# A gated delta rule between two recurrent layers on one core: eight sets of small products per block, issued as four pairs

## The chip, the cores and the metric

The kernel runs on one NeuronCore of a Trainium2 chip, in FP32. The metric is the device time of one execution in microseconds. Engines: PE is TensorE (its weight loads are shown apart, as PEld), ACT is ScalarE, DVE is VectorE, POOL is GpSimd, SP is SyncE, which issues the transfers.

## The reference

The input x is 8 x 1024 x 256 (B sequences, L places, D features). It goes through three residual steps: x + 0.5 ffn(ln(x)), then x + attn(ln(x)), then x + 0.5 ffn(ln(x)) with the same weights.

- `ffn` is a gated recurrence along the first axis, the 8 sequences: f = sigmoid(x wf' + c uf' + bf), i = sigmoid(x wi' + c ui' + bi), g = tanh(x wc' + c uc' + bc), c = f c + i g, and at the end tanh(x wo' + c_final uo' + bo). Each of the 1024 places is a lane of its own, so 8 steps in order are all that is sequential.
- `attn` is a gated delta rule along the 1024 places, for 8 x 16 heads of width 16: with k the RMS-normed input per head and v the negative of x W', per place S = lam S; S += beta k (v - k'S); o = k'S. Then a layer norm with weights over the sum of x W' and o.

## The kernel before, in words

**Blocks.** The 1024 places are cut into 8 blocks of 128 (NB). Block b holds 128 places on the partitions and 8 sequences, so one pass of the ffn recurrence over a block takes 8 steps (TILE, t = 0 to 7). A step of the ffn is 24 matrix products of 128x128 by 128x128 on PE (L445): 12 of the input (XMM), and 12 of the state (CMM), of which the last 12 wait for the state of the step before (`c_done`, L443). ScalarE makes the gates from PSUM (L462, L469), VectorE the new state (L484, L488, L490). An FP32 product shows in the trace as two PE records, so these 12 products are x24, a half of them x12.

**The chunked delta rule.** The recurrence of `attn` is made chunk by chunk, 16 places each. For a block, spread over the steps of the blocks behind it: transposes (lt, L665), the value products (v, L675), key rows and their transposes (kt, L684), gram products (g0 to g3, L704, 64 records each half), their transposes (gt, L839), a triangular solve on VectorE (inv1 to inv3, L790 and L793), transposes of the inverse (tt, L851), evicted by L822 on ScalarE and L801 on VectorE, and then the applied inverse: eight sets, ta0 to ta7 (L868). A set is 64 products of 32x32 by 32x32, 128 records, into one PSUM bank: sets with an even number go to bank 6 and are evicted by ScalarE (L829), those with an odd number to bank 7 and by VectorE (L808), both into `xs_out`, which SP stores at steps 0 (sets 0 to 3) and 4 (sets 4 to 7) (L914). The operands of a set stand on 32 partitions (`tok`); an even set and the odd one behind it use neighbouring strips of 32 partitions. The four products of an inner loop go to the four column strips:

```
for k in [4 * "abcd".index(part) + r for part in parts for r in range(4)]:
    for c in range(SETS):
        lane = SETS * (16 * kh + k) + c
        mm = pe.matmul(dst.ps[32 * c:32 * c + 32, 32 * k:32 * k + 32],
                       kv_of(n)[tok, lane, :], invT[tok, lane, :], ...)
```

**Two stages.** The first stage (`first_*`) runs blocks 0 to 5 of the first ffn (SOLO = 6), steps 0 to 47, up to about 474 us. The second (`second_*`) runs everything else, steps 48 to 130: the last two blocks of the first ffn, the 8 blocks of the second, and beside them the 64 hops of the delta rule's state, one per step from step 49 on. A hop is 32 products with the state (L1058), a copy by ScalarE (L1084), 32 products that make the new state (L1075), and five evictions into `zbd` (L1092 on ScalarE, L1099 on VectorE).

**The order around the change is a table written by hand.** `PERIOD` lists for each step t four parts, and for each part the items that go there, each with the number of blocks it lies behind the current one; `CLOSE` lists those behind step 7. All engines walk the same table, each doing its own share of an item, in the table's order. Where a part lies on PE differs by stage. In the first, part 0 lies between the two halves of XMM, part 1 behind XMM and ahead of CMM, part 2 between the halves of CMM, part 3 behind CMM; ScalarE and VectorE do the items of parts 0 to 2 ahead of their share of the step and those of part 3 behind it. In the second stage CMM is issued first, around the hop, and the four parts each stand behind 3 products of XMM of the next step; ScalarE and VectorE do all four parts behind their share of the step. At the block's end (`CLOSE`, the first stage) PE issues the output products h0 to h3 (L512), the term of the final state (L497) and the transposes of the next block (L405), and VectorE evicts them (L520, L526, L537), takes the statistics of the next layer norm (L83) and evicts the last gram sets (L630).

Sets 0 to 3 of a block come two blocks behind (steps 5, 5, 6 and the close), sets 4 to 7 three blocks behind (steps 1, 2, 2, 3). `fill_table` walks the same table and gives each PSUM bank the order in which it is filled; PE waits with `refill` for the bank's last eviction. A set waits for its bank, the first one also for `inv_cols`, the keys and the values (L856 to L861).

Of the kernel before, what the change touches and what calls it, by code (L numbers as in the profile page):

```python
# [130 lines left out]
class Bank:  # L131


    def __init__(self, k, ps, sem):
# [1 line left out]


PERIOD = {0: ([], [(2, "g3abcd")], [], [(1, "ln2_late")]),
# [7 lines left out]
CLOSE = ([], [(2, "ta3abcd")], [], [(1, "g2abcd")])  # L146
S_PIECES = (4, 5)
GRAMS = ("g0", "g1", "g2", "g3")
UNITS = tuple(f"ta{m}" for m in range(8))
# [26 lines left out]
def fill_table():  # L176
# [11 lines left out]
    def singles(banks, *keys):  # L188
        for key in keys:
            k = turn.get(banks, 0)  # L190
            put(banks[k % len(banks)], *key)
            turn[banks] = k + 1
# [6 lines left out]
    def four(name, n, js=range(4)):  # L199
        return [(name, n, j) for j in js]  # L200

    def piece(name, n):
        name, parts = unit_of(name)
        if not 0 <= n < NB or (parts and "a" not in parts):
            return
        if name[:2] in ("gt", "tt", "lt", "kt"):
            singles((4, 5), *four(name[:2], n, pair_of(name)))
        elif name == "al":
            singles((4, 5), ("al", n))
        elif name in ("v01", "v23"):  # L210
            singles((4, 5), *four("v", n, (0, 1) if name == "v01" else (2, 3)))
        elif name in GRAMS:
            pairs((6, 7), ("g", n, int(name[1])))
        elif name in UNITS:
            m = int(name[2])
            put(6 + m % 2, "ta", n, m)

    singles((4, 5), *four("fr1", 0))
    for b in range(SOLO):
# [8 lines left out]
        for part in range(4):  # L228
            if part == 2:
                singles((4, 5), *four("fr1", b + 1, (0, 1)))  # L230
            for behind, name in CLOSE[part]:
                piece(name, b - behind)
        singles((4, 5), ("ct1", b))
    for i in range(JOIN, END):
# [10 lines left out]
        if t == TILE - 1:  # L245
            for part in range(4):
                if part == 2 and n + 1 < NB:
                    singles((4, 5), *four(*(("fr1", b + 1) if n + 1 < 0 else ("fr2", n + 1)), (0, 1)))
                for behind, name in CLOSE[part]:
                    piece(name, b - behind)  # L250
# [5 lines left out]
def build(nc, x, weights, cols, rows, lanes, out):  # L256
    ctx = ExitStack()
    with ctx:
# [619 lines left out]
        def pieces(eng, b, names, prep, solve):  # L878

            for behind, name in names:  # L880
                if 0 <= b.n - behind < NB:
                    prep(eng, b.n - behind, name)
                    solve(eng, b.n - behind, name)
# [52 lines left out]
        def first_dve(dve):  # L936
            for b in blocks(SOLO):
                for t in range(8):
# [5 lines left out]
                    pieces(dve, b, PERIOD[t][3], prep_dve, solve_dve)  # L944
                pieces(dve, b, CLOSE[1], prep_dve, solve_dve)
                ff.dve_cterm(dve, b)
# [5 lines left out]
                ff.dve_h(dve, b, 3)  # L952
                pieces(dve, b, CLOSE[3], prep_dve, solve_dve)
                ff.dve_x(dve, b, 2)
# [9 lines left out]
        def first_pe(pe):  # L964
            for b in blocks(SOLO):
# [13 lines left out]
                ff.pe_h(pe, b, 0)  # L979
                pieces(pe, b, CLOSE[0], prep_pe, solve_pe)  # L980
                ff.pe_h(pe, b, 1)
                pieces(pe, b, CLOSE[1], prep_pe, solve_pe)
                ff.pe_front(pe, b.ahead(1), (0, 1))
# [571 lines left out]
```

## Time and profile before

| | us |
|---|---|
| Median of 3 runs | 1371.61 |
| Runs | 1363.80 to 1374.17 |
| The profiled execution, its own time | 1371.25 |
| Its span, first to last instruction | 1369.5 |
| PE busy / PEld busy | 1263.5 / 1167.3 |
| DVE busy / ACT busy / POOL busy | 878.1 / 666.4 / 269.5 |

The durations come from the one profiled execution, taken by the hardware profiler. Busy time is the union of an engine's instructions; matmuls are pipelined and their ends modelled, so the distance from one start to the next says more than a duration. In brackets behind a row of the timeline stands how long the engine was idle before it and who released it; "issue" means that nothing in the profile ended the wait. The granted clock (PEclk) is TensorE's, as a share of full speed. A row of the windows gives the stretch, its length, then busy time and number of instructions for PE, PEld, DVE, ACT and POOL, the granted clock, the mean busy share of the DMA engines and GB/s. A row of a queue gives packets, MB and the share of time of the 16 DMA engines.

### The profile page before, as it was taken

How to read it: one execution, taken by the hardware profiler on the slowest of the kernel's cores; microseconds unless marked ns; L12 is line 12 of the kernel's file. 1: busy time of each engine (PE TensorE's matmuls, PEld its weight loads, DVE VectorE, ACT ScalarE, POOL GpSimd, SP SyncE). 2: the span in 40 equal slices, each digit the busy share in tenths (PEclk: the TensorE clock that was granted, in tenths of full speed). 3: DMA queues.
4: the chain of work that ended last, by engine and by line, in shares of the span. 5: the costliest groups of instructions: out<-in, count | busy, mean ns of one | idle time of the engine just before them, and what ended most of it. 6: DMA issues, size and time to landing. Idle time of an engine off the chain costs nothing.

```text
span 1369.5 us, 58093 instructions
## 1 busy us (share of the span) xinstructions
PE 1263.5 (92%) x25763; PEld 1167.3 (85%) x25763; DVE 878.1 (64%) x2147; ACT 666.4 (49%) x1623; POOL 269.5 (20%) x350
## 2 busy tenths in 40 slices
PE   6999999999999999998898899899899999999896
PEld 5989998989989888787777788888789989898886
DVE  3656886868879676577658764953445546464632
ACT  3244444454434535544463555355365756655432
POOL 0113112021311111112503230230130405050500
PEclk9999999999999999999998999999999999999999
DMA  4010201122121223242214223324234233333000
GB/s 146 1 62 32 65 33 66 64 80 73 42 80 50 102 68 92 67 140 66 83 47 162 65 74 117 92 77 138 73 95 150 65 112 102 109 102 108 1 32 31
DMA packets 72378, 108.36 MB, mean 79 GB/s; under 512 B 12352, under 2 KB 49472, under 8 KB 70080
## 3 DMA queue, kind: packets, MB, share of 16 engines
q1 hardware_dynamic: 72128, 104.65, 23.9%
q8 instruction: 203, 3.33, 1.0%
q14 instruction: 47, 0.39, 0.1%
HBM read 53.74 MB, written 50.86 MB: 76 GB/s over the span
## 4 chain that ended last, share of the span: by engine, by line
PE 67%; DVE 18%; ACT 8%; issue 5%; DVEq 0%; ACTq 0%
PE ps L445 37%; PE ps L512 7%; PE ps L868 5%; PE ps L1058 4%; PE ps L1075 3%; ACT gates L462 3%; PE ps L675 3%; ACT zbd L1092 2%; DVE prod L790 2%; DVE inv L793 2%; DVE ln_bn L83 2%; PE ps L405 2%; PE ps L704 1%; DVE hs L526 1%; DVE ffn_rows L537 1%
## 5 line engine op out<-in xcount | busy, mean ns | idle before, releaser
L445 PE MATMUL ps<-cst,wt 128*128 128x128 f32 x2688 | 348.7, 282 | 3.5 <-DVE cst L490 3.4
L445 PEld LDWEIGHTS ps<-cst,wt 128*128 128x128 f32 x2688 | 318.7, 194 | 14.6 <-DVE cst L490 4.1
L445 PE MATMUL ps<-ffn_rows,wt 128*128 128x128 f32 x2304 | 295.7, 281 | 10.8 <-DVE hs L526 4.1
L445 PEld LDWEIGHTS ps<-ffn_rows,wt 128*128 128x128 f32 x2304 | 275.9, 194 | 20.8 <-issue 13.2
L462 ACT ACTIVATE gates<-ps,colv 128x128 f32<-128x128 f32 x448 | 128.0, 369 | 188.7 <-PE ps L445 188.5
L484 DVE TENSOR_TENSOR fc<-gates,cst 128x256 f32<-128x256 f32 x112 | 56.1, 501 | 223.5 <-ACT gates L462 223.5
L1161 POOL TENSOR_TENSOR ffn_rows<-ffn_rows,rowv 128x256 f32<-128x256 f32 x64 | 52.0, 851 | 351.3 <-DMA ffn_rows<-x_scratch 351.3
L1092 ACT ACTIVATE zbd<-ps,mask 32x256 f32<-32x256 f32 x252 | 104.0, 458 | 10.7 <-PE ps L1075 7.6
L868 PE MATMUL ps<-inv_cols,kv 32*32 32x32 f32 x8192 | 88.7, 194 | 18.5 <-issue 16.9
L868 PEld LDWEIGHTS ps<-inv_cols,kv 32*32 32x32 f32 x8192 | 79.2, 104 | 30.5 <-issue 20.9
L445 PE MATMUL ps<-kg_rows,wt 128*128 128x128 f32 x768 | 95.1, 278 | 6.6 <-DVE hs_more L526 3.5
L445 PEld LDWEIGHTS ps<-kg_rows,wt 128*128 128x128 f32 x768 | 89.2, 192 | 10.3 <-issue 5.8
L512 PE MATMUL ps<-wt,ffn_rows 128*128 128x256 f32 x384 | 91.8, 384 | 5.8 <-DVE hs L526 3.0
L1084 ACT COPY e<-ps 128x512 f32<-128x512 f32 x64 | 37.5, 585 | 118.9 <-PE ps L1058 118.9
L1058 PE MATMUL ps<-zbd,xsb 128*32 128x64 f32 x4096 | 86.3, 239 | 7.4 <-issue 7.3
L83 DVE BATCH_NORM_STATS2 ln_bn<-ffn_rows 128x6 f32<-128x256 f32 x256 | 86.6, 411 | 9.2 <-DMA ffn_rows<-x 8.7
L1058 PEld LDWEIGHTS ps<-zbd,xsb 128*32 128x32 f32 x4096 | 75.9, 149 | 19.3 <-issue 14.2
L488 DVE TENSOR_TENSOR ig<-gates 128x256 f32<-128x256 f32 x128 | 61.3, 479 | 44.7 <-ACT gates L469 41.7
L101 POOL TENSOR_SCALAR key_rows<-ffn_rows,ln_stats 128x256 f32<-128x256 f32 x64 | 39.2, 628 | 256.5 <-PE ps L839 207.1
L512 PEld LDWEIGHTS ps<-wt,ffn_rows 128*128 128x128 f32 x384 | 70.0, 190 | 17.5 <-ACT gates L462 4.2
L650 POOL TENSOR_TENSOR kg_rows<-key_rows,g_tok 128x512 f32<-128x512 f32 x32 | 47.2, 1501 | 188.1 <-DVE key_rows L604 188.1
L1099 DVE TENSOR_TENSOR zbd<-ps,mask 64x1024 f32<-64x1024 f32 x63 | 76.2, 1210 | 7.6 <-PE ps L1075 7.6
(123 smaller groups left out, 1793.7 us busy)
## 6 DMA issues: line engine op xcount, KB each, us to landing
xs_scratch<-xs_out SPq DMA_DIRECT2D x32, 512.0 KB, 3.5
xsb<-xs_scratch SPq DMA_DIRECT2D x256, 64.0 KB
ffn_rows<-x SPq DMA_DIRECT2D x32, 256.0 KB, 3.6
x_scratch<-ffn_rows SPq DMA_DIRECT2D x32, 256.0 KB, 2.8
kg_scratch<-kg_rows SPq DMA_DIRECT2D x32, 256.0 KB, 2.8
kgb<-kg_scratch SPq DMA_DIRECT2D x256, 32.0 KB, 2.3
e_scratch<-e SPq DMA_DIRECT2D x256, 32.0 KB
ffn_rows<-e_scratch SPq DMA_DIRECT2D x8, 1024.0 KB
```

The source lines that it names most:

```text
L83: link(dve.bn_stats(stats[:, b, 0:6], src[:, b, :]))
L445: mm = pe.matmul(banks[g][:, col:col + P], wt[:, w, k, m * P:(m + 1) * P], rhs, start=(x in (0, FI)), stop=(k == KT - 1 and (t == 0 or x > ...
L462: a = act.activation(gates[q][:, g, m * P:(m + 1) * P], fi[:, g * D + m * P:g * D + (m + 1) * P], ACT.Sigmoid, bias=bias[:, g, m:m + 1])
L484: a = dve.tensor_tensor(fc, gates[q][:, 0, :], cst, ALU.mult)
L488: dve.tensor_tensor(ig, gates[q][:, 1, :], gates[q][:, 2, :], ALU.mult).then_inc(self.products, 1)
L512: mm = pe.matmul(h_b[j][:, e * D:(e + 1) * D], self.xnT[b.n % len(self.xnT)][:, k, 2 * j + e, :], wt[:, WO, k, :], start=(e == 0 and k == ...
L650: pool.tensor_tensor(kg_rows.rearrange("p (b h d) -> p b h d", h=H, d=HD)[:, 2 * r:2 * r + 2, :, :], key_rows.rearrange("p (b h d) -> p b ...
L868: mm = pe.matmul(dst.ps[32 * c:32 * c + 32, 32 * k:32 * k + 32], kv_of(n)[tok, lane, :], invT[tok, lane, :], start=True, stop=True, skip_g ...
L1058: mm = pe.matmul(E_BANK[32 * g:32 * g + 32, 64 * kk:64 * kk + 64], xs_cols[:, k // C, k % C, C * a:C * a + 2 * C], zbd[:, k, :], start=Tru ...
L1092: act.activation(zbd[rows, C:2 * C, cols], S_BANKS[rows, :, cols], ACT.Copy, scale=mask4[rows, c:c + 1]).then_inc(z_done, 1)
L1099: dve.tensor_tensor(zbd[0:64, 0:C, :].rearrange("p k (c d) -> p k c d", c=SETS), S_BANKS[0:64, :, :].rearrange("p k (c d) -> p k c d", c=S ...
L1161: pool.tensor_tensor(xt[p][:, r, :], xt[p][:, r, :], rowv[:, 2, :], ALU.add).then_inc(post_done, 1)
```

## The change

The sets are issued two at a time, at one place of a step. Sets 4 and 5 come in part 1 of step 1, sets 6 and 7 in part 2 of step 2, sets 0 and 1 in part 2 of step 5, sets 2 and 3 in part 1 of step 6. The block's close and step 3 have none left. Nothing else of the table is changed; the products, the banks, the evictions and the transfers are the same ones, and each engine's share of an item moves with it.

```
 PERIOD = {0: ([], [(2, "g3abcd")], [], [(1, "ln2_late")]),
-          1: ([(2, "gt0")], [(3, "ta4abcd"), (1, "lc2")], [], [(2, "gt1"), (2, "inv1"), (1, "apply")]),
-          2: ([(3, "ta5abcd")], [], [(3, "ta6abcd")], [(1, "lt0"), (2, "inv2")]),
-          3: ([(1, "lt1"), (1, "square")], [(3, "ta7abcd")], [(2, "al")], [(1, "v01"), (2, "inv3")]),
+          1: ([(2, "gt0")], [(3, "ta4abcd"), (3, "ta5abcd"), (1, "lc2")], [], [(2, "gt1"), (2, "inv1"), (1, "apply")]),
+          2: ([], [], [(3, "ta6abcd"), (3, "ta7abcd")], [(1, "lt0"), (2, "inv2")]),
+          3: ([(1, "lt1"), (1, "square")], [], [(2, "al")], [(1, "v01"), (2, "inv3")]),
           4: ([(1, "v23"), (1, "sums")], [(1, "rms")], [(2, "tt0")], [(2, "tt1"), (1, "key")]),
-          5: ([(1, "keys")], [(2, "ta0abcd")], [], [(2, "ta1abcd"), (-1, "ln1")]),
-          6: ([(1, "kt0")], [(2, "ta2abcd"), (1, "km0")], [], [(1, "kt1"), (-1, "lc1")]),
+          5: ([(1, "keys")], [], [(2, "ta0abcd"), (2, "ta1abcd")], [(-1, "ln1")]),
+          6: ([(1, "kt0")], [(2, "ta2abcd"), (2, "ta3abcd"), (1, "km0")], [], [(1, "kt1"), (-1, "lc1")]),
           7: ([(1, "g0abcd"), (-1, "ap0")], [], [(1, "g1abcd"), (-1, "ap1")], [(1, "km1")])}
-CLOSE = ([], [(2, "ta3abcd")], [], [(1, "g2abcd")])
+CLOSE = ([], [], [], [(1, "g2abcd")])
```

## Rows read from the trace of the kernel before

**Rows 1.** The page: busy time by engine, and the instruction queue.

```profile
PE 1263.5 (92%) x25763; PEld 1167.3 (85%) x25763; DVE 878.1 (64%) x2147; ACT 666.4 (49%) x1623; POOL 269.5 (20%) x350
...
q8 instruction: 203, 3.33, 1.0%
```

**Rows 2.** Windows: first stage from 226 us, then the stretch with sets and hops.

```profile
226.00:474.00 248.00, 239.22 (x5275) 223.71 (x5274) 197.72 (x468) 113.73 (x267) 47.80 (x60) 1.00 0.20 69
474.00:985.00 511.00, 459.72 (x12092) 415.70 (x12096) 334.03 (x749) 255.49 (x589) 100.06 (x124) 0.95 0.29 91
```

**Rows 3.** Waits of PE: total us, times, longest.

```profile
PE ps L868 <- issue: 16.9, 14, 3.4
...
PE ps L851 <- DVE inv_cols L801: 8.7, 4, 3.2
PE ps L1058 <- issue: 7.3, 6, 2.6
```

**Rows 4.** Timeline of PE, second stage, sets 5 and 6: start, us, instruction.

```profile
501.36 0.27 PE L868 MATMUL ps<-inv_cols,kv 32*32 32x32 f32 x9 [0.27 <-issue]
501.56 1.60 PE L445 MATMUL ps<-ffn_rows,wt 128*128 128x128 f32 x12
503.09 1.10 PE L868 MATMUL ps<-inv_cols,kv 32*32 32x32 f32 x107
505.38 0.38 PE L868 MATMUL ps<-inv_cols,kv 32*32 32x32 f32 x21 [1.19 <-issue]
```

**Rows 5.** The same for the last block's sets 5 and 6.

```profile
965.35 0.45 PE L868 MATMUL ps<-inv_cols,kv 32*32 32x32 f32 x31 [0.85 <-issue]
965.73 1.60 PE L445 MATMUL ps<-ffn_rows,wt 128*128 128x128 f32 x12
967.27 0.92 PE L868 MATMUL ps<-inv_cols,kv 32*32 32x32 f32 x85
971.56 0.85 PE L868 MATMUL ps<-inv_cols,kv 32*32 32x32 f32 x43 [3.38 <-issue]
```

**Rows 6.** Timeline of PE, first stage, sets 5 and 6.

```profile
237.64 1.29 PE L868 MATMUL ps<-inv_cols,kv 32*32 32x32 f32 x128
238.85 1.60 PE L445 MATMUL ps<-ffn_rows,wt 128*128 128x128 f32 x12
240.30 1.50 PE L445 MATMUL ps<-cst,wt 128*128 128x128 f32 x12
241.73 0.55 PE L868 MATMUL ps<-inv_cols,kv 32*32 32x32 f32 x40
242.59 0.95 PE L868 MATMUL ps<-inv_cols,kv 32*32 32x32 f32 x88 [0.31 <-issue]
```

**Rows 7.** Timeline of PE, first stage, step 4, away from the sets.

```profile
346.64 1.50 PE L445 MATMUL ps<-cst,wt 128*128 128x128 f32 x12
347.98 1.06 PE L851 MATMUL ps<-ident,inv 128*128 128x128 f32 x8
```

**Rows 8.** Window at half clock, columns as in rows 2, to 755.73 us.

```profile
748.91:755.73 6.82, 6.82 (x155) 6.25 (x142) 6.62 (x11) 2.45 (x4) 4.36 (x6) 0.50 0.06 13
```

**Rows 9.** Timeline of PE, second stage, behind two other sets.

```profile
732.43 2.93 PE L445 MATMUL ps<-ffn_rows,wt 128*128 128x128 f32 x12
735.15 1.10 PE L839 MATMUL ps<-ident,key_rows 128*128 128x128 f32 x8
...
748.68 1.15 PE L868 MATMUL ps<-inv_cols,kv 32*32 32x32 f32 x77 [3.13 <-issue]
```

**Rows 10.** Timeline, first stage: the new state of step 1, its products in step 2.

```profile
320.81 0.67 DVE L490 TENSOR_TENSOR cst<-fc,ig 128x256 f32<-128x256 f32 x1
...
324.34 1.50 PE L445 MATMUL ps<-cst,wt 128*128 128x128 f32 x12
```

**Rows 11.** Timeline, first stage, block's end: VectorE's first item, and PE behind its last.

```profile
385.45 0.42 DVE L520 TENSOR_TENSOR cterm<-ps,rowv 128x256 f32<-128x256 f32 x1 [2.85 <-PE ps L497]
...
396.02 1.14 PE L839 MATMUL ps<-ident,key_rows 128*128 128x128 f32 x8 [1.43 <-DVE key_rows L630]
```

## The prediction

> **What bounds the kernel now.** I read the page's busy rows first, then the windows by stage, then TensorE's timeline, and last the chain of waits for the two kinds of idle time that it has.
>
> TensorE (PE) is busy 1263.5 us of a span of 1369.5 us; the next engine, VectorE, 878.1 us [rows 1]. The share is high in both stages: 239.2 of 248 us (96%) in the first stage from 226 us on, where the sets run without hops, and 459.7 of 511 us (90%) in the stretch where sets and hops run together [rows 2]. So PE's own order sets the time, and a moved item on PE costs or gives what it adds to or takes from PE's queue. What fills PE's idle time differs: in the first stage it is a few waits for VectorE and ScalarE at a block's seam, in the second it is first of all "issue" before the lines of the change (L868, 16.9 us in 14 waits) and of the hop (L1058, 7.3 us in 6) [rows 3]. "Issue" means that the engine had no semaphore to wait for. The change lies on that line, so this is what I look at closest.
>
> What stands behind it: the instruction queue brought 203 packets and 3.33 MB [rows 1], 16.4 KB a packet. PE ran 25763 matmuls and 25763 weight loads, 51526 instructions; 3.33 MB over these is 64.6 bytes each, and 51526 / 203 is 254. So I read that queue as PE's own code, and a packet as a page of about 256 instructions, 128 matmul records with their loads. One set is 128 records, so a set is one page of code.
>
> The idle times have exactly that spacing. PE idles for issue inside a set at 501.36, then runs 9 + 12 + 107 = 128 records, and idles for issue again until 505.38 [rows 4]. It resumes at 965.35, runs 31 + 12 + 85 = 128, and idles until 971.56 [rows 5]. In both a set is followed by only 12 ordinary records and then the next set. A page was entered at 501.36 and the next one only at 505.38: 4.0 us; the other took 6.2 us (965.35 to 971.56). In the first stage the wait at 242.59 lies 40 + 12 + 12 + 64 records behind a point halfway through the set at 237.64, about 238.2: 4.4 us a page, and there only 0.31 us of it shows, because 24 ordinary records lie between the two sets [rows 6]. I take from this: the next page is asked for when the present one is entered, and is there about 4 us later (6 where transfers are dense); a page that is run faster than that ends in a wait.
>
> **The change part by part.** Per block eight sets become four pairs, 32 merges in all.
>
> *Merged switches (gain).* A group of 12 ordinary records takes 1.34 us between its own kind (346.64 to 347.98) [rows 7]; 1.43 us when a set follows (240.30 to 241.73) and 1.45 after a set (238.85 to 240.30), and the set itself 1.21 us (237.64 to 238.85) [rows 6]. A lone set so costs 1.21 + 0.09 + 0.11 = 1.41 us. The second set of a pair has ordinary records on neither side: between 1.0 us (it also loses the hand-over at its end) and 1.21. A merge saves 0.2 to 0.4, I take 0.3: 32 x 0.3 = 10 us. The step from one set to the next in another row strip and PSUM bank is not in this trace; if it cost as much as a switch the gain is 0, so this term is 0 to -13 us.
>
> *A whole page inside a pair (loss).* A pair is 256 records, 512 instructions, so wherever the pages fall at least one lies wholly in the pair. It is run in 1.2 us and the next page comes 4.0 us after its entry: 2.8 us of wait. PE's queue takes code a little ahead of the array, so I use 2.5 in the first stage, where also fewer transfers run (69 GB/s against 91 [rows 2]). Its bounds are 0.3 us (the wait at 242.59, were the queue to cover the rest) and 5.0 (6.2 - 1.2). First stage: sets 0 to 3 of four blocks and sets 4 to 7 of three, 8 + 6 = 14 pairs: +35 us. The waits that it has now there (0.3 us seen at L868) are worth 1 us.
>
> Second stage: 18 pairs. There the page price is 4.0 to 6.2, and the pair stands among two hop groups of 64 records each; I take 3.1 us a pair, 56 us. Against that stands what is there now: L868 16.9 less the 0.3 of the first stage and L1058 7.3 make 24 us [rows 3], since sets 5 and 6 and sets 0 and 1 are already 12 records apart in this stage, near to a pair. Net +32. PE now waits 8.7 us in all for VectorE's eviction at L801 [rows 3], at the end of its solve of the block; a PE that is late finds part of this gone: -4. Bounds of this term: +5 (the near pairs are as bad as pairs, only steps 1 and 6 get worse, by 1 us each) to +60 (5.0 a pair).
>
> *The clock (loss).* Over 474 to 985 the granted clock is 0.95 [rows 2], and it falls to 0.50 for some 3.4 us at a time after waits of this kind: the stretch from 748.91 on is at 0.50 [rows 8], right after the wait of 3.13 us that ended at 748.68, and the group of 12 that starts at 732.43 behind another set needs 2.72 us, to 735.15 [rows 9], where 1.45 is usual [rows 6]. The first stage has 1.00 [rows 2]. Half speed costs 1.3 us for one such group, and 1.7 for a whole stretch of 3.4 us. With a pair and its wait of 2.5 us in one piece I expect most pairs to end so. New are 14 in the first stage and 9 in the second (steps 1 and 6; the other 9 pairs stand where near pairs stand now and have such stretches already). Not each will fall on ordinary records: 23 x 0.9 = 21 us. Bounds 0 and 23 x 1.7 = 39.
>
> *Covers that get shorter (nothing).* Set 5 leaves step 2 ahead of the recurrent products. Now the state is written at 321.48 (320.81 + 0.67) and those products start at 324.34 [rows 10]; without the set's 1.41 us some 1.4 us of that remains, and the eviction of set 5, which now comes ahead of VectorE's coefficients in step 1, must fit in there. Set 3 leaves the block's end; VectorE starts there with the term at 385.45, which waits 2.85 us for PE, and works from there up to the gram eviction that PE awaits at 396.02 [rows 11], so PE and VectorE move ahead together and that wait stays at 1.43 us. Sets 1 and 7 are evicted a half step earlier, between waits for the gates. Were one of these covers gone, I put it at 1 us a block, 8 us. No DMA moves: the stores of the sets stay at steps 0 and 4.
>
> *Sum against the profiled run:* 1371.25 us (span 1369.5 and 1.75 around it), which is the median of the runs, 1371.61, to 0.03%. 1371.25 - 10 + 35 - 1 + 32 - 4 + 21 = 1444 us.
>
> **A rule that speaks against this.** The Trainium skill, "Runtime: NRT & Kernel Launch", section on instruction fetch mechanics, has the same page, 16 KiB or 256 instructions, fetched while the present one runs, but says that crossing a page is mostly hidden, and gives PE room for 2048 instructions. By it the pair's 512 instructions would be there ahead and only the merges would count. The waits of rows 4 and 5, one page apart, say otherwise.
>
> **The rivals.**
> 1. *Merges alone: faster.* PE's code is ahead by more than a pair, and the waits at L868 have another cause that goes with the hop. For it: the first stage runs its lone sets with almost no issue wait. Against it: 128 records between two waits, twice, and a wait at 242.59 without a hop near. It decides from the point where two pages are ready at a pair's start. Time: 1371.25 - 10 = 1361. The page of the skill named above is the rule for this one.
> 2. *Waits, but short and without the clock.* PE takes code far enough ahead that a pair waits 1.0 to 1.5 us, and such waits leave the clock at 1.00. For it: near pairs 12 records apart wait as little as 1.19 us (at 505.38). Against it: those 12 records gave PE 1.5 us of other work, and others wait 3.38 us all the same [rows 4, 5]. Time, with 5 us for a clock that falls here and there: 1371.25 - 10 + 32 x 1.2 - 4 + 5 = 1401.
> 3. *Pages at 6 us everywhere.* The fetch is as slow in steps 1, 2 and 6 of each stage, where the block's loads and stores are issued, as at 971.56. Time: 1371.25 - 10 + 14 x 3.8 + 18 x 4.5 - 24 - 4 + 30 = 1497.
> 4. *A tie.* Waits of some 0.3 us a pair eat the merges' gain: 1371.25 - 10 + 10 = 1371.
>
> **How the numbers follow.** The forecast has 0.74 (own range 1410 to 1475), rival 1 0.03, rival 2 0.12, rival 3 0.08, rival 4 0.03. About 1% is what a measurement can tell here, so faster is below 1357.9 and slower above 1385.3: 0.03 faster, 0.03 the same, 0.94 slower. The range leaves out most of rivals 1, 3 and 4 and the low end of rival 2: 1396 to 1484 us.
>
> **What would show it right or wrong.** In the changed profile: issue waits before L868 in nearly all 32 pairs, 2 to 3 us each, 70 to 100 us together, also before 474 us, where there is 0.3 now; successive waits 128 records apart; the first stage's granted clock below 1.00; a block of the first stage with four pairs some 10 us longer. Of the merge: 12-record groups between the old places of the sets back at 1.34 us. It is wrong if the pairs run through in 2.3 us without a break, or if the added time stands before L445 with VectorE as the releaser (a cover gone), or if the waits come but are under 1.5 us.

## The result and the profile after

The changed kernel takes 1464.9 us (median of 4 runs, 1461.8 to 1470.5) against 1370.3 us: a ratio of 1.0725, 95% interval 1.0683 to 1.0767. It is slower, as forecast, and by more: 95 us where 73 were forecast, inside the range of 1396 to 1484 us.

The page of the changed kernel answers to [rows 1]: the same numbers of instructions, the same 203 packets of code, PE busy for 1307.4 us instead of 1263.5, in a span that is 99.2 us longer.

```profile
span 1468.7 us, 58093 instructions
...
PE 1307.4 (89%) x25763; PEld 1214.5 (83%) x25763; DVE 864.8 (59%) x2147; ACT 668.7 (46%) x1623; POOL 267.8 (18%) x350
...
q8 instruction: 203, 3.33, 0.9%
```

The waits of PE (total us, times, longest), to set beside [rows 3]:

```profile
PE ps L868 <- issue: 75.7, 34, 4.4
...
PE ps L851 <- DVE inv_cols L801: 8.7, 4, 3.2
...
PE ps L665 <- DVE zbd L1099: 5.0, 3, 2.2
...
PE ps L1058 <- issue: 2.7, 2, 1.7
```

Issue waits inside the sets went from 16.9 us in 14 to 75.7 us in 34. The first stage alone (25 us to the first hop at 536.7) shows it without anything beside it, since it had one wait of 0.3 us there:

```profile
PE ps L868 <- issue: 30.6, 15, 2.6
```

Two of its pairs in PE's timeline: first set 5 beside set 4, with the ordinary records behind it, then sets 6 and 7.

```profile
337.85 2.42 PE L868 MATMUL ps<-inv_cols,kv 32*32 32x32 f32 x228
342.62 0.64 PE L868 MATMUL ps<-inv_cols,kv 32*32 32x32 f32 x28 [2.35 <-issue]
343.19 3.14 PE L445 MATMUL ps<-cst,wt 128*128 128x128 f32 x13
...
353.20 1.54 PE L868 MATMUL ps<-inv_cols,kv 32*32 32x32 f32 x159
357.17 1.02 PE L868 MATMUL ps<-inv_cols,kv 32*32 32x32 f32 x97 [2.43 <-issue]
358.12 2.93 PE L445 MATMUL ps<-cst,wt 128*128 128x128 f32 x12
360.84 1.38 PE L665 MATMUL ps<-ident,key_rows 128*128 128x128 f32 x8
```

The 256 records of a pair come as 228 + 28 or 159 + 97: no break where the second set begins, at 128, but one at another place each time. From one of the 14 long waits of this stage to the next PE runs 256, 762, 256, 507, 255, 763, ... records, close to a multiple of 127 or 128 each time (51526 instructions in 203 packets are 254 each, 127 records with their loads).

The trace also keeps the packets of the instruction queue one by one, 16384 bytes each. In this stage such a packet ends inside each of the 14 long waits, and PE resumes 1.2 to 1.6 us behind its end. The wait that ends at 342.62 has a packet from 340.39 to 341.31, the wait that ends at 357.17 one from 354.77 to 355.86. So the spacing is not the only sign that these waits are for code.

The group of 12 behind the second pair takes 2.72 us (358.12 to 360.84), where a group behind a set takes 1.45 in [rows 6]. The windows say why: at both pairs a stretch at half clock follows, which in the first of them begins inside the wait. The last two rows are the block of the first stage around them, 98.8 us, and the same block before, 83.4 us: 15.4 us more for four pairs.

```profile
341.00:347.80 6.80, 5.17 (x49) 5.11 (x50) 3.31 (x21) 0.79 (x4) 0.00 (x0) 0.50 0.01 2
358.10:361.50 3.40, 3.40 (x26) 3.38 (x17) 1.18 (x2) 1.55 (x6) 0.00 (x0) 0.50 0.02 5
324.90:423.70 98.80, 87.83 (x1791) 83.08 (x1790) 65.04 (x159) 39.13 (x90) 15.21 (x20) 0.91 0.16 56
...
302.00:385.40 83.40, 81.18 (x1790) 75.98 (x1790) 66.88 (x158) 38.52 (x90) 15.94 (x20) 1.00 0.19 67
```

**Where the 99 us are.** The windows split the two traces, the kernel before first, at the first hop. In the first stage (25 us to the first hop):

```profile
25.00:481.70 456.70, 440.14 (x7828) 414.10 (x7827) 344.59 (x865) 205.66 (x501) 84.51 (x108) 1.00 0.16 56
```

```profile
25.00:536.70 511.70, 466.31 (x7811) 441.84 (x7809) 335.80 (x865) 206.64 (x497) 82.25 (x108) 0.93 0.14 50
```

It is 55.0 us longer, 28.8 us of it PE idle (511.7 - 466.3 against 456.7 - 440.1) and 26.2 us PE busy with the same work. From the first hop to the last set, again before and after:

```profile
481.70:982.20 500.50, 449.51 (x11839) 406.20 (x11841) 324.70 (x713) 251.26 (x578) 100.06 (x124) 0.95 0.30 92
```

```profile
536.70:1074.00 537.30, 459.05 (x11792) 417.87 (x11791) 320.86 (x711) 247.16 (x567) 96.93 (x119) 0.90 0.27 85
```

Idle time rose from 51.0 to 78.3 us, by 27.3. (The last set now stands a step earlier than before, so the lengths of these windows aren't compared; from the first hop to the end the span is 44.2 us longer: 1468.7 - 536.7 against 1369.5 - 481.7.) Together: 56 us of idle time and 43 us of slower work.

### The profile page after: what moved, and what is told of

It reads as the page before. It is cut to its first block, busy times and chain, and to the rows that moved or that the text cites. A ratio compares the mean times of both kernels' runs of the same rounds, so it can differ in the third digit from the quotient of the medians.

```text
span 1468.7 us, 58093 instructions
## 1 busy us (share of the span) xinstructions
PE 1307.4 (89%) x25763; PEld 1214.5 (83%) x25763; DVE 864.8 (59%) x2147; ACT 668.7 (46%) x1623; POOL 267.8 (18%) x350
## 4 chain that ended last, share of the span: by engine, by line
PE 68%; DVE 16%; issue 8%; ACT 7%; DVEq 0%; ACTq 0%
PE ps L445 39%; PE ps L512 6%; PE ps L868 5%; PE ps L1058 4%; PE ps L1075 3%; PE ps L675 3%; ACT gates L462 2%; DVE prod L790 2%; DVE inv L793 2%; ACT zbd L1092 2%; DVE ln_bn L83 2%; PE ps L704 1%; PE ps L405 1%; DVE hs L526 1%; PE ps L684 1%
## 5 line engine op out<-in xcount | busy, mean ns | idle before, releaser
L445 PE MATMUL ps<-cst,wt 128*128 128x128 f32 x2688 | 372.1, 294 | 3.4 <-DVE cst L490 3.4
L445 PEld LDWEIGHTS ps<-cst,wt 128*128 128x128 f32 x2688 | 341.3, 205 | 14.5 <-DVE cst L490 4.1
L445 PE MATMUL ps<-ffn_rows,wt 128*128 128x128 f32 x2304 | 304.7, 287 | 10.9 <-DVE hs L526 4.1
L445 PEld LDWEIGHTS ps<-ffn_rows,wt 128*128 128x128 f32 x2304 | 286.9, 201 | 20.1 <-issue 13.0
L484 DVE TENSOR_TENSOR fc<-gates,cst 128x256 f32<-128x256 f32 x112 | 52.3, 467 | 250.1 <-ACT gates L462 250.1
L868 PE MATMUL ps<-inv_cols,kv 32*32 32x32 f32 x8192 | 91.4, 199 | 75.7 <-issue 75.7
L868 PEld LDWEIGHTS ps<-inv_cols,kv 32*32 32x32 f32 x8192 | 83.4, 109 | 83.6 <-issue 79.5
L445 PE MATMUL ps<-kg_rows,wt 128*128 128x128 f32 x768 | 97.9, 284 | 6.6 <-DVE hs_more L526 3.5
L445 PEld LDWEIGHTS ps<-kg_rows,wt 128*128 128x128 f32 x768 | 91.9, 197 | 10.3 <-issue 5.8
L1058 PEld LDWEIGHTS ps<-zbd,xsb 128*32 128x32 f32 x4096 | 77.5, 151 | 16.0 <-issue 11.6
L1058 PE MATMUL ps<-zbd,xsb 128*32 128x64 f32 x4096 | 87.7, 244 | 2.9 <-issue 2.7
L1099 DVE TENSOR_TENSOR zbd<-ps,mask 64x1024 f32<-64x1024 f32 x63 | 76.2, 1209 | 6.2 <-PE ps L1075 6.2
```

Of the source, the lines that this page charges most:

```text
L445: mm = pe.matmul(banks[g][:, col:col + P], wt[:, w, k, m * P:(m + 1) * P], rhs, start=(x in (0, FI)), stop=(k == KT - 1 and (t == 0 or x > ...
L484: a = dve.tensor_tensor(fc, gates[q][:, 0, :], cst, ALU.mult)
L1058: mm = pe.matmul(E_BANK[32 * g:32 * g + 32, 64 * kk:64 * kk + 64], xs_cols[:, k // C, k % C, C * a:C * a + 2 * C], zbd[:, k, :], start=Tru ...
L1099: dve.tensor_tensor(zbd[0:64, 0:C, :].rearrange("p k (c d) -> p k c d", c=SETS), S_BANKS[0:64, :, :].rearrange("p k (c d) -> p k c d", c=S ...
```

## The experiments

Kernels in which a table differs by stage have a second copy of `PERIOD` and `CLOSE`, and so 9 is added to the line numbers: L877 is L868, L1067 is L1058, L454 is L445, L674 is L665, L1108 is L1099. "First stage" below is 25 us to the first hop.

**The pairs of one stage alone.** Do the two stages add up? First with the changed table for blocks 0 to 5 only (the code in outline):

```
 for b in range(SOLO): ... PERIOD[t][part], CLOSE[part]      # changed table
 for i in range(JOIN, END): ... PERIOD2[t][part], CLOSE2[part]   # old table
```

Expected: 

> The changed table for blocks 0 to 5 (first stage), the old one behind them: 14 of the 32 pairs. Code pages and clock: each of the 14 pairs waits 2.1 to 2.6 us for code and is followed by a half-clock stretch, as in the changed kernel's first stage, where the first hop came 55 us later; 1370 + 55 = 1425 us, and the second stage as before, with its 24 us of issue waits. If the pairs of the first stage shift what the second stage waits for, it is off this by more than 8 us.

Measured: 1425.9 us (ratio 1.041, 1.037 to 1.046), the first hop at 535.5 us against 481.7. In its first stage:

```profile
PE ps L877 <- issue: 30.4, 15, 2.5
```

The other way round, `PERIOD` old and `PERIOD2` changed:

Expected: 

> The old table for blocks 0 to 5, the changed one behind them: 18 of the 32 pairs. If the two stages add up, this has what the first stage's pairs do not explain: 1370 + 97 - 55 = 1412 us, first stage at clock 1.00 without an issue wait, waits at L868 some 45 us.

Measured: 1413.7 us (1.030, 1.024 to 1.036). The two extras, 56 and 44 us, make 100 where the whole change has 95. So the stages add up within the intervals, which are 7 to 8 us wide on either side: 14 pairs cost 4.0 us each and 18 pairs 2.4 us each, and no effect of one stage on the other is seen. In the second kernel the waits inside the sets behind the first hop are close to the changed kernel's: 44 us against 45.

**Half the code in each set.** In `solve_pe`, with the old table and then with the changed one:

```
-for k in [4 * "abcd".index(part) + r for part in parts for r in range(4)]:
+for k in [4 * "abcd".index(part) + r for part in parts if part in "ab" for r in range(4)]:
```

A set is then 64 records, and a pair of them 128; these kernels leave out the other half of the applied inverse. Expected of the sets one by one: 

> The old table, and every set computes only its first half (32 products, 64 records, half a page of code); the other half of the applied inverse is left out. Code pages: 64 sets are 0.55 us shorter (-35), and since two sets 12 records apart are now less than a page together, nearly all issue waits of the second stage go (-20) and with them most half-clock stretches (-15): 1300 us. Rival (two sets close to each other disturb the array or PSUM itself, whatever their code): only the 35 us go, 1335 us, and the waits at L868 stay near 17 us.

Expected of the pairs: 

> The changed table with the same half sets: a pair is one page of code instead of two; the other half of the applied inverse is left out. Code pages: hardly any page lies wholly in a pair, so the waits at L868 fall from 76 us to under 15, and the merges show alone: 10 us less than the half sets one by one, about 1290 us. Rival (the step from one set to the next in another row strip and bank is what waits): 32 waits of 2.3 us and their clock stay, some 90 us above the half sets one by one, about 1390 us.

Measured: 1323.2 us one by one, 1323.7 us as pairs (ratios to before 0.966, 0.961 to 0.971, and 0.968, 0.962 to 0.973). The rival's 1390 us for the pairs is excluded: with the same places, the same 32 steps to another row strip and bank and half the code, the 95 us are gone. This alone does not say whether the code or the halved work took them away; the four sets in a row below do. PE's timeline of the half-size pairs, two of them with the records around them:

```profile
302.66 1.50 PE L445 MATMUL ps<-ffn_rows,wt 128*128 128x128 f32 x12
304.10 1.31 PE L868 MATMUL ps<-inv_cols,kv 32*32 32x32 f32 x128
305.34 2.94 PE L445 MATMUL ps<-cst,wt 128*128 128x128 f32 x24
...
311.70 1.50 PE L445 MATMUL ps<-cst,wt 128*128 128x128 f32 x12
313.13 1.31 PE L868 MATMUL ps<-inv_cols,kv 32*32 32x32 f32 x128
314.37 1.60 PE L445 MATMUL ps<-cst,wt 128*128 128x128 f32 x12
```

A pair of half sets runs in 1.24 us without a break, 0.03 us more than one whole set of 128 records in [rows 6]: the change of strip and bank costs nothing to speak of. For the worth of a merge I compare the first stages, one by one and then as pairs:

```profile
25.00:465.90 440.90, 425.23 (x6031) 399.17 (x6030) 343.50 (x865) 205.16 (x501) 84.42 (x108) 1.00 0.17 58
```

```profile
25.00:462.20 437.20, 419.38 (x6019) 395.97 (x6017) 341.12 (x863) 204.19 (x495) 84.31 (x108) 1.00 0.17 58
```

PE is busy 5.85 us less over 14 merges, 0.42 us each, and 2.1 us of that is waited again. But my expectation of both kernels missed by 23 and 34 us, and the two were to differ by 10: in the second stage the gain does not reach the end. From the first hop on the pairs even take 7.2 us more than the sets one by one (859.6 against 852.4). These waits of PE for VectorE in the kernel one by one have grown most:

```profile
PE ps L665 <- DVE zbd L1099: 19.4, 3, 9.1
...
PE ps L844 <- DVE zbd L1099: 5.8, 1, 5.8
```

Before, L665 waited 3.7 us for that and L844 1.0, so 20.5 us are new. In the second stage a PE that comes early to step 3 waits for VectorE's share of the hop, which stands behind the solve in VectorE's queue (L790 and L793 from 716.2 to 725.2 ahead of L1099 at 725.47, where the wait of 9.1 us ends). In three of the four blocks in which the half sets wait there the old kernel does too, for 0.9 to 2.7 us. My reading is that its issue waits ahead of that place (2.78 us in step 2 of one block, 3.13 in that of the next) only shortened this wait and cost nearly nothing; no run takes them away by themselves.

**A near pair: 12 ordinary records between the two sets.** First stage only.

```
-          1: ([(2, "gt0")], [(3, "ta4abcd"), (3, "ta5abcd"), (1, "lc2")], [], ...
+          1: ([(2, "gt0")], [(3, "ta4abcd"), (1, "lc2")], [(3, "ta5abcd")], ...
...
+          2: ([], [(3, "ta6abcd")], [(3, "ta7abcd")], ...
+          5: ([(1, "keys")], [(2, "ta0abcd")], [(2, "ta1abcd")], ...
+          6: ([(1, "kt0")], [(2, "ta2abcd"), (1, "km0")], [(2, "ta3abcd")], ...
```

(The line with a minus is the changed kernel's.)

Expected: 

> First stage only: the same four places, but 12 ordinary records between the two sets of a pair (sets 4 and 5 in parts 1 and 2 of step 1, and so on); the second stage as before. Code pages: the page now holds 12 ordinary records and takes 2.4 us instead of 1.1, so the wait is 3.6 - 2.4 = 1.2 us instead of 2.4: 14 x 1.2 = +17, and a clock that falls in half of the cases +9: 1396 us. Rival (sets in a row wait for the array): no wait and no fall of the clock in the first stage, 1370 us.

Measured: 1386.3 us (1.012, 1.008 to 1.017), the first hop 19.0 us later than before. The rival's 1370 lies outside the interval. The waits of the first stage, and one of its near pairs:

```profile
PE ps L877 <- issue: 12.3, 15, 1.7
```

```profile
333.81 1.29 PE L877 MATMUL ps<-inv_cols,kv 32*32 32x32 f32 x128
335.03 1.60 PE L454 MATMUL ps<-cst,wt 128*128 128x128 f32 x12
336.56 0.45 PE L877 MATMUL ps<-inv_cols,kv 32*32 32x32 f32 x31
338.06 1.02 PE L877 MATMUL ps<-inv_cols,kv 32*32 32x32 f32 x97 [1.05 <-issue]
```

The wait stands at 128 + 31 records, as in the pair at 353.20, and has 1.05 us instead of 2.43: the 12 records took 1.4 us of it. So the wait is about what is missing to a fixed time per page, as expected (0.9 us a pair against 1.2). The clock did less than expected: the first stage has 0.99, with three stretches of 3.4 us at half clock at 14 pairs.

```profile
25.00:500.70 475.70, 447.00 (x7821) 419.57 (x7819) 338.85 (x865) 206.68 (x501) 82.85 (x108) 0.99 0.16 54
```

**Four sets in a row.** First stage only, sets 4 to 7 in part 2 of step 2 and sets 0 to 3 in part 1 of step 6:

```
+          2: ([], [], [(3, "ta4abcd"), (3, "ta5abcd"), (3, "ta6abcd"), (3, "ta7abcd")], ...
+          6: ([(1, "kt0")], [(2, "ta0abcd"), (2, "ta1abcd"), (2, "ta2abcd"), (2, "ta3abcd"), (1, "km0")], ...
```

Expected: 

> First stage only, four sets in a row at two places of a block (sets 4 to 7 in part 2 of step 2, sets 0 to 3 in part 1 of step 6), 7 places in all; the second stage as before. Code pages: 512 records are four pages, so three pages are run in 1.1 us each and each is followed by a wait of 2.4 us: 21 waits, 50 us of idle time before the first hop against 29 with the 14 pairs; with some 18 us of half clock and 6 us for the merges the time is 1370 + 62 = 1432 us. Rival (one wait for each place where sets stand in a row, however many): 7 waits, 16 us, with 12 us of half clock 1370 + 22 = 1392 us.

Measured: 1428.1 us (1.045, 1.042 to 1.048). The rival's 1392 is excluded. The waits of its first stage, and one of the seven places:

```profile
PE ps L877 <- issue: 41.8, 21, 2.7
```

```profile
346.77 1.54 PE L877 MATMUL ps<-inv_cols,kv 32*32 32x32 f32 x159
350.51 1.85 PE L877 MATMUL ps<-inv_cols,kv 32*32 32x32 f32 x128 [2.21 <-issue]
354.24 1.85 PE L877 MATMUL ps<-inv_cols,kv 32*32 32x32 f32 x128 [1.88 <-issue]
357.69 1.51 PE L877 MATMUL ps<-inv_cols,kv 32*32 32x32 f32 x97 [1.60 <-issue]
```

This is the clearest picture of the mechanism. There are 21 waits at 7 places, as the pages have it, and exactly 128 records, 256 instructions, between two of them. In each of the 21 a packet of the instruction queue ends 1.3 to 1.5 us before PE resumes. From one wait's end to the next 3.73 us pass (350.51 to 354.24) and 3.45 us (354.24 to 357.69). The waits were smaller than my 2.4 us, since the later ones find the sets themselves slower (1.85 us for 128 records, not 1.31): that fills part of the same time. That the total came within 4 us of the expectation is luck in part: in the first stage idle time rose by 40 us instead of 50, and PE's busy time by 20.5 instead of 12.

```profile
25.00:542.20 517.20, 460.67 (x7825) 436.31 (x7824) 344.81 (x865) 207.14 (x501) 84.44 (x108) 0.91 0.14 50
```

**Four half sets in a row.** The same places with the half sets.

Expected: 

> The same places with half sets (32 products each; the other half of the applied inverse is left out): four half sets in a row are 256 records, as much code as one pair of whole sets. Code pages: one wait of 2.4 us at each of the 7 places, 17 us of idle time in the first stage, each with a half-clock stretch (some 10 us together), less the merges: 1323 + 22 = 1345 us. If the number of sets in a row counted and not their code, it would be three waits at each place, as with the whole quads: 50 us, 1385 us; with none at all 1318 us.

Measured: 1355.6 us (0.991, 0.988 to 0.994), against 1323.2 for the half sets one by one. The waits of its first stage and one of its places:

```profile
PE ps L877 <- issue: 11.4, 7, 2.0
```

```profile
328.67 1.31 PE L877 MATMUL ps<-inv_cols,kv 32*32 32x32 f32 x128
330.22 0.45 PE L877 MATMUL ps<-inv_cols,kv 32*32 32x32 f32 x31 [0.23 <-ACT xs_out L838]
332.50 1.37 PE L877 MATMUL ps<-inv_cols,kv 32*32 32x32 f32 x97 [1.83 <-issue]
333.79 2.93 PE L454 MATMUL ps<-cst,wt 128*128 128x128 f32 x12
```

Seven issue waits, one per place, with four sets in each: the code counts, not the sets. A pair of whole sets, which is as much code, has one wait as well. As two sets use each bank here, the third and fourth sets also wait for an eviction: the third 0.2 us each time (1.6 in all, L838), the fourth at three places (3.2 us in all, L817). The time is 10 us above the expectation. This stage is 29.4 us longer than with half sets one by one (first hop 495.3 against 465.9); 15.3 us of that is idle time (31.0 against 15.7, with the 4.8 us for the banks in it) and 14.1 us PE busy for longer, with a half-clock stretch at all seven places.

**Sets spread wider than before.** The opposite of the change, second stage only:

```
+          0: ([], [(2, "g3abcd")], [], [(1, "ln2_late"), (3, "ta4abcd")]),
+          1: ([(2, "gt0")], [(1, "lc2")], [(3, "ta5abcd")], ...
+          2: ([], [(3, "ta6abcd")], [], ...
+          3: ([(1, "lt1"), (1, "square")], [(3, "ta7abcd")], ...
+          5: ([(1, "keys")], [(2, "ta0abcd")], [], [(-1, "ln1")]),
+          6: ([(1, "kt0"), (2, "ta1abcd")], [(1, "km0")], [], [(2, "ta2abcd"), (1, "kt1"), ...
```

Expected: 

> The opposite of the change, in the second stage only: no two sets close to each other (set 4 in part 3 of step 0, 5 in part 2 of step 1, 6 in part 1 of step 2, 7 in part 1 of step 3, 0 in part 1 of step 5, 1 in part 0 and 2 in part 3 of step 6, 3 at the close). Code pages: the issue waits of the second stage fall from 26 to about 10 us and the half-clock stretches from 49 us to about 20: 1370 - 16 - 12 = 1342 us. If code is not the cause: 1370 us, within 1%.

Measured: 1390.9 us (1.015, 1.010 to 1.019): a miss by 49 us, and slower. Its waits from the first hop to the last set:

```profile
PE ps L1067 <- issue: 18.9, 10, 4.1
PE ps L674 <- DVE zbd L1108: 18.1, 3, 8.7
...
PE ps L853 <- DVE zbd L1108: 5.6, 1, 5.6
...
PE ps L877 <- issue: 2.4, 5, 0.7
```

The waits left the sets (2.4 us, from 16.6) and went to the hop (18.9, from 6.9): I had moved sets to the end of steps, next to the hop's own dense code, and a page doesn't ask whose code it is. PE also waits 23.7 us for VectorE's `zbd` here, 19 us more than before and most of the added time: the same wait that the half sets showed.

**A smaller attempt.** Second stage only, sets 0 and 1 one part earlier in step 5:

```
-          5: ([(1, "keys")], [(2, "ta0abcd")], [], [(2, "ta1abcd"), (-1, "ln1")]),
+          5: ([(1, "keys"), (2, "ta0abcd")], [], [(2, "ta1abcd")], [(-1, "ln1")]),
```

Expected: 

> An attempt to beat the old order, second stage only: sets 0 and 1 of step 5 stand one part earlier (parts 0 and 2 instead of 1 and 3), so that 6 more ordinary records lie between set 1 and the next hop's code. Code pages: of the 5 us of waits at or behind set 1 in this stage 2 to 3 go, and a half-clock stretch or two: 1370 - 5 = 1365 us, hardly to be told from no change.

Measured: 1369.5 us, ratio 1.001 (0.999 to 1.004): no difference. No order that was tried beats the old one.

## Why the prediction was right, and where it was off

**The merges** gain what was said, somewhat more: 0.42 us each against 0.3, 13 us in all if the second stage's are worth the same. That the step between the two sets might cost a switch was a bound; the half-size pairs show 0.03 us for it. The sign that the forecast named has come too. At the old place of set 5, between the halves of XMM, the 24 records now take 2.68 us, 1.34 for 12:

```profile
349.09 2.84 PE L445 MATMUL ps<-ffn_rows,wt 128*128 128x128 f32 x24
351.77 1.50 PE L445 MATMUL ps<-cst,wt 128*128 128x128 f32 x12
```

**The whole page inside the pair** is shown. All 14 pairs of the first stage wait, the break stands on the page's spacing and not where the sets meet, a packet of code ends shortly before each wait does, half the code takes the waits away, 12 ordinary records between the sets shorten them by the time of these records, four sets in a row have three waits and four half sets have one. The size was near: the changed kernel's idle time is 28.8 us longer in the first stage (forecast 35 less 1) and 27.3 in the second (forecast 32 less 4), 56 against 62. A pair of the first stage waits 2.2 us where I took 2.5. In the second stage the waits at L868 and L1058 went from 24 to 48 us, 2.7 a pair against 3.1, so 24 us net against 32; the price is lower net because the old kernel pays there already. The 4 us that PE's lateness was to take from its wait for VectorE's eviction (L801) did not come: 8.7 us in 4 waits, before and after.

**The clock** is the term that was mis-sized: 21 us forecast. In the first stage PE's busy time rose by 26.2 us although the merges took 5.85 away, so 32 us go to slower work; in the second stage 44.2 us less 27.3 of idle time and plus 7.5 for its 18 merges leave 24. That makes 56 us, 2.7 times the forecast and above its upper bound of 39. The clock's part is what is left when the rest is taken away, not measured by itself; the rows agree with it. The granted clock of 0.93 over 511.7 us means 0.07 x 511.7 / 0.5 = 72 us at half speed, 5.1 us a pair, where I had counted at most one stretch of 3.4 a pair and 0.9 us for it. All 14 pairs have such a stretch, and at six of them it is 6.8 us long, as at 341.00. By the same reckoning the second stage went from 50 to 107 us at half speed, more than nine new pairs at 5.1 us would add, so the pairs that I took as paid for already fell deeper as well. 56 - 21 is 35 us too little, of which the waits (6 too much) and the merges (3 too little) take back 9: 26, the distance from the forecast 73 to the profile's 99. So the total is inside the range although this term is not inside its own, because the terms for the waits came out lower and the merges gained more.

**The covers** held: PE's waits for the new state (L445 for `cst`, 2.8 us in the first stage in both traces) and for the gram eviction (L839, 5.7 us in both, 1.4 at the longest) didn't move. "Time before L445 with VectorE as the releaser" did not come.

**The rivals.** Merges alone and a tie were wrong: their only support, that lone sets in the first stage run without waits, is what the page time makes of 24 ordinary records between two sets. The short waits without the clock had the wrong size in both parts. Pages at 6 us everywhere came at a few places only (the last pair waited 4.42 us). There the packet itself is as short as elsewhere but starts late: 0.94 us long and 3.5 us behind the entry of the page before (counted back 128 records), where the median of the first stage's 14 is 0.9 us. In the old kernel's wait of 3.38 us it is 0.94 us long and 3.8 us late. What held it up is not shown.

**The rule of the Trainium skill** ("Runtime: NRT & Kernel Launch", instruction fetch mechanics) is borne out in the page of 16 KiB or 256 instructions (packets of 16384 bytes, 128 records apart) and in fetching the next page while one runs. Its remarks that the crossing is mostly hidden, and that PE's store has room for 2048 instructions, don't fit a wait at each page of the four sets in a row: here a page that runs in 1.3 to 1.9 us is followed by 1.4 to 2.7 us of wait.

**What stays open:** whether the clock falls for the wait, for the small products around it, or only for both together. The old kernel has a wait of 2.10 us between ordinary products before 474.29 with a granted clock of 1.00 on both sides; half-size pairs, with one issue wait of 0.2 us in all, don't lower it in the first stage (1.00); the pairs of the changed kernel, with waits of 1.5 to 2.6 us, do at all 14. The length of the wait alone does not decide it: of two near pairs with waits of 1.69 and 1.70 us only the first is followed by half clock, while the four half sets in a row, with issue waits of 1.1 to 2.0 us, have it at all seven places. But those also wait for their banks, and no run sets a wait among small products against one among ordinary ones at the same length.

## What to carry to other kernels

Count the instructions on PE, not only its time: each record of a small product is two instructions with its weight load, and where 256 instructions in a row ran faster than that, the next 256 came mostly 3.2 to 4 us after them here, and up to 6.2 us in the stage with more transfers. So dense small products want ordinary, long ones between them, about 24 records of 128x128x128 per 128 small ones (with 24 the first stage had one wait of 0.3 us, with 12 it had 0.9 us a pair). Saving 0.4 us by putting two dense groups side by side was a loss of 2.2 us of wait and 2.3 us of slower clock in the first stage. And before such waits are removed, look what the engine would wait for next: with half the code most of them were gone, and PE waited 20.5 us more for VectorE instead.

## What I had not expected of the hardware

A wait of 1.5 to 2.6 us inside 2.5 us of small products came with half clock at all 14 pairs of the first stage, for 3.4 or 6.8 us, in some of them from inside the wait on, while waits of 0.9 us at the same places left 0.99. At half clock the small products slow down too: 128 records show 1.85 us instead of 1.31. That fills part of the next wait for code (2.21, 1.88 and 1.60 us in the four sets in a row), so the two losses don't simply add.
